# A gated long convolution with a feed-forward branch on one core: channel-innermost V and GC1, mixing and output in one block, the test on far lags turned round

## What is computed

```
proj = xn @ in_proj_w + in_proj_b
v = proj[..., :d]
for i in range(2):                         # two orders
    ctrl = proj[..., (i + 1) * d:(i + 2) * d]
    h = implicit_filter(...)               # a filter of 2048 lags per channel
    v = causal_conv(v, h)
    xc = conv3(ctrl); v = v * xc * sigmoid(xc @ gate_w[i] + gate_b[i])
attn = v @ out_proj_w + out_proj_b
r = relu(xn @ Wfc.T + gate * low_rank);  ffn = (r * r) @ Wproj.T
out = x + attn + ffn
```

## Time and profile before

| | |
|---|---|
| median of three runs | 960.2 us |
| profiled execution | 957.4 us, its span 955.8 us |
| mixing stage | about 372 to 870 us |
| output stage | about 870 to 956 us |
| TensorE busy | 863.9 us, 90% |
| VectorE, ScalarE busy | 631.3 us, 479.1 us |
| GpSimd busy | 248.7 us |
| DMA | 152.8 MB, mean 160 GB/s |

### The profile page before, as it was taken

The page is one execution under the profiler, slowest core; times in us unless marked ns, Lnnn a source line. Parts: engine busy times, 40 slices in busy tenths (PEclk is TensorE's granted clock), DMA queues, the critical chain, the costliest instruction groups (busy, mean ns, idle before and its releaser), DMA issues. The chain is left out here.

```text
span 955.8 us, 26466 instructions
## 1 busy us (share of the span) xinstructions
PE 863.9 (90%) x9972; PEld 718.4 (75%) x9973; DVE 631.3 (66%) x1025; ACT 479.1 (50%) x678; POOL 248.7 (26%) x268
## 2 busy tenths in 40 slices
PE   6846999999999973999999999999999999972995
PEld 3324888888888863888888888888888888862895
DVE  6882799898998973456555565565555655651885
ACT  5413677777777773333443343444434343334662
POOL 1022464664646601011121121111111111110111
PEclk9977899999999997999999999999999999985998
DMA  6272323324233129676778868778777687693897
GB/s 185 65 252 106 117 100 123 141 88 159 105 119 145 68 95 292 119 172 160 164 146 195 181 154 172 145 174 183 176 167 162 148 183 172 127 196 86 249 332 275
DMA packets 86705, 152.84 MB, mean 160 GB/s; under 512 B 12981, under 2 KB 62278, under 8 KB 85382
## 3 DMA queue, kind: packets, MB, share of 16 engines
q1 hardware_dynamic: 74902, 109.01, 47.2%
q0 software_dynamic: 11616, 42.21, 13.4%
q10 hardware_dynamic: 144, 1.05, 0.3%
HBM read 102.83 MB, written 49.41 MB: 159 GB/s over the span
## 5 line engine op out<-in xcount | busy, mean ns | idle before, releaser
L1080 PEld LDWEIGHTS py<-vwin,lead 64*64 64x64 f32 x5120 | 134.0, 134 | 35.8 <-issue 35.8
L965 DVE TENSOR_TENSOR r_lo<-r,r_hi 128x512 fp32r<-128x512 f32 x128 | 107.6, 840 | 78.8 <-ACT r_hi L1012 78.8
L1080 PE MATMUL py<-vwin,lead 64*64 64x128 f32 (+4 forms) x5120 | 147.8, 266 | 12.8 <-issue 12.7
L1012 ACT ACTIVATE r_hi<-r 128x512 fp32r<-128x512 f32 x128 | 80.8, 631 | 153.7 <-DVE r L960 153.7
L1009 ACT ACTIVATE r<-pf 128x512 f32<-128x512 f32 x128 | 76.5, 598 | 137.2 <-PE pf L412 132.7
L1061 PE MATMUL pp<-wproj,r_hi 128*128 128x256 f32 x512 | 135.9, 299 | 3.4 <-DVE r_lo L965 2.4
L1061 PE MATMUL pp<-wproj,r_lo 128*128 128x256 f32 x512 | 127.8, 282 | 0.0
L451 POOL TENSOR_SCALAR lead<-lead,norms 128x256 f32<-128x256 f32 x64 | 113.8, 1788 | 3.4 <-POOL norms L445 3.4
L1061 PEld LDWEIGHTS pp<-wproj,r_hi 128*128 128x128 f32 x512 | 96.9, 189 | 19.2 <-DVE r_lo L965 5.7
L611 DVE SCALAR_TENSOR_TENSOR xc<-ctrl,taps,xc 128x512 f32<-128x512 f32 x128 | 96.8, 776 | 18.8 <-ACT xc L683 18.1
L410 PE MATMUL pf<-tokens,split_a 128*128 (+1 forms) x256 | 101.3, 396 | 0.4 <-issue 0.4
(11 more groups left out here) (158 smaller groups left out, 1607.1 us busy)
## 6 DMA issues: line engine op xcount, KB each, us to landing
lead<-filters SPq DMA_DIRECT2D x128, 320.0 KB, 5.9
xnT_hbm<-split_b SPq DMA_DIRECT2D x32, 512.0 KB, 3.1
tokens<-xnT_hbm POOLq DMA_DIRECT2D x32, 512.0 KB, 7.0
lead<-in_attn_x SPq DMA_DIRECT2D x16, 512.0 KB, 3.8
gc_hbm<-xc SPq DMA_DIRECT2D x16, 512.0 KB, 2.6
xb<-in_attn_x POOLq DMA_DIRECT2D x16, 512.0 KB, 7.2
xf_hbm<-xb POOLq DMA_DIRECT2D x16, 512.0 KB, 3.8
GC<-gc_hbm SPq DMA_DIRECT2D x32, 256.0 KB, 7.4
```

What stands on the lines that cost most here:

```text
L965: dve.tensor_tensor(r_lo[j][:, :], r[j][:, :], r_hi[j][:, :].bitcast(F32), ALU.subtract).then_inc(r_split, 1)
L1012: act.activation(r_hi[j][:, :], r[j][:, :], ACT.Copy).then_inc(r_hi_done, 1)
L1080: last = pe.matmul(py[g % 2][q * BW:(q + 1) * BW, side, l, :, A:NB], tile[rows, q * PAIR + l, j * BW:(j + 1) * BW], vwin[g % 2][rows, q, l ...
```

## The change

`V` and `GC1` become [128, batch, block, channel slot 128]. The stores of the projection stage are then contiguous, the group accesses of the mixing stage touch single words 512 bytes apart (two adjacent channel slots on each of two sides). The copy to `ys` is gone: TensorE transposes straight out of `V`.

`output_stage` is gone as a block of its own; its code goes to the end of `mix_stage`, without a barrier. Its buffers are laid over others: `pT` over `py`, `po` over `pf` and `pp`, the halves of `wo` over the first token buffer, those of `yg` over `split_b` and the second token buffer, `yg` in `GC1`. New waits order that: `y_out`, `relu_done` and `xf_ready` on TensorE, `fc_mm` on ScalarE. VectorE's gate of chunk 0 goes ahead of the last `r_lo`. TensorE's loop over the output's chunks is unrolled.

`load_output` goes from behind the last T load to the start of the last chunk's four groups, ahead of the T load of group 60.

SP and TensorE test `tail < 1` and have the usual loops in the If branch.

```diff
@@ SP, T loads @@
+                        if g == 0 and isinstance(it, int) and it == NCH - 1:
+                            sp.wait_ge(y_out, GROUPS // ORDERS + 2)
+                            sp.wait_ge(xf_saved, 16 * SLOTS)
+                            load_output(sp)
                         if not first or g:
                             wait_alone(sp, group_mm, G + 1, sp_passed)
                             load(T[g % 2], 0, NEAR, T_loaded[g % 2])
...
-            with sp.If(tail > 0):
+            def stages(far):
                 for order in range(ORDERS):
-                    loads(order, True)
+                    loads(order, far)
+                sp.wait_ge(xf_saved, 16 * NCH)
+                for c in (SLOTS, SLOTS + 1):
+                    gates(c, c % SLOTS)
...
+            with sp.If(tail < 1):
+                stages(False)
             with sp.Else():
-                for order in range(ORDERS):
-                    loads(order, False)
-            sp.wait_ge(y_out, GROUPS // ORDERS + 2)
-            sp.wait_ge(xf_saved, 16 * SLOTS)
-            load_output(sp)
+                stages(True)
@@ mix_stage @@
-        Vs = V[:, :, :, :].rearrange("p (b c) n a -> p b c (n a)", b=SIDES)
-        Gs = GC1[:, :, :, :].rearrange("p (b c) n a -> p b c (n a)", b=SIDES)
+        Vs = V[:, :, :, :].rearrange("p n a (b c) -> p b c (n a)", b=SIDES)
+        Gs = GC1[:, :, :, :].rearrange("p n a (b c) -> p b c (n a)", b=SIDES)
@@ VectorE @@
+                    if last and g == GPI - 1:
+                        gated(0, 0)
                     low(it, 2 * g + 1)
...
+            yg_low(0, 0)
+            gated(1, 1)
             scale(NCH - 1)
             add(NCH - 1)
+            yg_low(1, 1)
+            for c in (2, 3):
+                output(c, c)
...
@@ TensorE @@
+            def stages(far):
+                for order in range(ORDERS):
+                    mixed(order, far)
+                pe.wait_ge(y_out, GROUPS + 2)
+                transposed(0, 0)
+                transposed(1, 1)
+                proj(NCH - 1, HT - 2)
+                proj(NCH - 1, HT - 1)
+                pe.wait_ge(wo_split, 1)
+                pe.wait_ge(relu_done, NCH * HT + 2)
+                projected(0, 0)
+                pe.wait_ge(xf_ready, NCH + 1)
+                for c in range(2, NCH):
+                    transposed(c, c % SLOTS)
+                    projected(c - 1, (c - 1) % SLOTS)
+                projected(NCH - 1, (NCH - 1) % SLOTS)
+
+            with pe.If(tail < 1):
+                stages(False)
+            with pe.Else():
+                stages(True)
```

More of the change, by code:

```diff
@@ L811, in channels, with mix_stage @@
     return m * (GPI * PAIR) + g * PAIR
[L814 removed]
+def mix_stage(nc, load_output, xf_saved, gc2_saved, x, filters, fc_hi, fc_lo, proj_t, xnT_hbm, xf_hbm, out_b, scales, flag, V, GC1, T, wfc, xm, split, T_loaded, w_in, xn_loaded, load_T, load_tokens,
+              out, load_gates, load_sum, ident, gc2, xf, wo, yg, gc2_loaded, xf_loaded, wo_in):
     with ExitStack() as ctx:
@@ L939, in _ @@
             save_xf(NCH - 1)
+            with pool.Fori(0, NCH // SLOTS) as m:
+                for j in range(SLOTS):
+                    c = m * SLOTS + j
+                    wait_alone(pool, out_ready, c + 3, pool_passed)
+                    pool.dma_start(out_tiles[bass.ds(c, 1)].rearrange("c p i d -> (c p) i d"), xf[j]).then_inc(out_saved[j], 16)
+            for j in range(SLOTS):
+                pool.wait_ge(out_saved[j], 16 * NCH // SLOTS)
         @block.vector
@@ L965, in low, with blocks, gated, yg_low @@
                 dve.tensor_tensor(r_lo[j][:, :], r[j][:, :], r_hi[j][:, :].bitcast(F32), ALU.subtract).then_inc(r_split, 1)
+            def blocks(rows):
+                return rows.rearrange("p k (t j) -> p k t j", j=BW)
+            def gated(c, j):
+                dve.wait_ge(yT_mm, c + 1)
+                dve.wait_ge(gc2_loaded[j], (c - j) * (16 * KT // SLOTS) + 16 * KT)
+                dve.tensor_tensor(blocks(yg[j % 2]), pT[j % 2].rearrange("p t k j -> p k t j"), blocks(gc2[j]), ALU.mult).then_inc(yg_ready, 1)
+            def yg_low(c, j):
+                i = j % 2
+                dve.wait_ge(yg_hi_done, c + 1)
+                dve.tensor_tensor(ygs[i][1], yg[i], ygs[i][0].bitcast(F32), ALU.subtract).then_inc(yg_split, 1)
+            def summed(c, j):
+                dve.wait_ge(out_mm, c + 3)
+                dve.wait_ge(xf_loaded[j], (c - j) * (16 // SLOTS) + 16)
+                dve.tensor_tensor(xf[j], po[j % 2], xf[j], ALU.add).then_inc(out_ready, 1)
+            def output(c, j):
+                gated(c, j)
+                summed(c - 2, (j + 2) % SLOTS)
+                yg_low(c, j)
             def body(order, m, it, first):
+                last = isinstance(it, int) and it == NCH - 1
                 for g in range(GPI):
@@ L984, in body @@
                     square(it, 2 * g + 1)
+                    if last and g == 1:
+                        dve.wait_ge(wo_hi_ready, 1)
+                        dve.tensor_tensor(wos[1], wo, wos[0].bitcast(F32), ALU.subtract).then_inc(wo_split, 1)
+                    if last and g == GPI - 1:
+                        gated(0, 0)
                     low(it, 2 * g + 1)
             for order in range(ORDERS):
-                lagging(dve, order, lambda m, it, first: body(order, m, it, first))
+                lagging(dve, order, lambda m, it, first: body(order, m, it, first), True)
+            yg_low(0, 0)
+            gated(1, 1)
             scale(NCH - 1)
             add(NCH - 1)
+            yg_low(1, 1)
+            for c in (2, 3):
+                output(c, c)
+            with dve.Fori(1, NCH // SLOTS) as m:
+                for j in range(SLOTS):
+                    output(m * SLOTS + j, j)
+            for c in (NCH - 2, NCH - 1):
+                summed(c, c % SLOTS)
         @block.scalar
@@ L1022, in body @@
                     activate(it, 2 * g)
+                    if last and order == ORDERS - 1 and g == 0:
+                        act.wait_ge(wo_in, 16 * KT)
+                        act.wait_ge(fc_mm, (NCH - 1) * HT + HT)
+                        act.activation(wos[0], wo, ACT.Copy).then_inc(wo_hi_ready, 1)
                     activate(it, 2 * g + 1)
@@ L1029, in _, with high @@
                 body(order, ITERS - 1, ITERS * order + ITERS - 1, True)
+            def high(c, i):
+                act.wait_ge(yg_ready, c + 3)
+                act.wait_ge(out_mm, c + 1)
+                act.activation(ygs[i][0], yg[i], ACT.Copy).then_inc(yg_hi_done, 1)
+            act.wait_ge(fc_mm, NCH * HT + HT)
+            with act.Fori(0, NCH // 2) as m:
+                for i in range(2):
+                    high(m * 2 + i, i)
         @block.tensor
```

209 lines of the change are left out of this document (49 added, 160 removed).

## The result

The changed kernel takes 974.4 us (median of four, 973.3 to 977.2) where the kernel before takes 959.9: ratio 1.0149, 95% interval 1.0111 to 1.0188. It is slower by 1.5%. I had forecast 958 and a range of 943 to 970.

The account below looks back on a forecast made before the run. TensorE was taken to bound the mixing, TensorE and DMA nearly level to bound the output, with a gap between. Terms -22.3 + 17.5 - 6 + 8.5 = -2.3 from 960.2 gave 958 us, range 943 to 970.

Parts of the forecast that it names:

- Part 1: Mixing and output joined without a barrier: matmuls of chunk 2 start 23.9 us earlier, -22.3 us in all, bounds -18 and -24.
- my list: Mixing's end: operations from the last V operation (849.80) to the last feed-forward add (861.0), then its save, landed about 865.
- At the 313 GB/s of the earlier trace that is 67 us: Joined output: 21.0 MB of loads and stores left after the last save take 67 us, so DMA ends at 935.
- Between the two I take 933.5: End of the joined output: taken between 935 by DMA and 931.9 by the compute pace, giving -22.3 us.
- Part 2: Output's inputs loaded ahead of group 60's T load: TensorE stands 16 us, plus 1.5 at low clock; +17.5 us.
- my sum: Ahead of group 60: from the moved load's first issue at 808.4 to group 60's T load landed at 838.5.
- rival (a): Group 60's T load isn't late, through queue order or a higher read rate; 940, or 949 with half the stall; chance 0.16.
- Part 3: Mixing's start: the usual loops fall through, without the 7.7 us branch; group 1 starts 6.5 us earlier; -6 us.
- Landing after 7.9 as the slowest T load, at 382: Mixing's start: T load of group 1, issued at about 374.5, lands at 382, so group 1 starts 6.5 us earlier.
- Part 4: V and GC1 with channel innermost: 0.5 us more per V operation, paid at 15 chunk closings; +8.5 us, bounds 0 and +19.
- Rival (c): Mixing's start keeps its stall, since the code behind the test isn't fetched ahead either; 964 us; chance 0.07.

Follow-up runs that it names:

- join alone: Changed kernel with the old layout, the old test and the slots loaded behind the last T load, so only the join remains: 944.0 us, ratio 0.9813.
- thin gates: Changed kernel with slots loaded behind the last T load and gate loads from chunk 4 on cut to an eighth of their bytes: 943.8 us, ratio 0.9821.
- layout alone: Kernel before with only the layout of V and GC1 changed, ys still copied: 969.9 us, ratio 1.0080.
- test alone: Kernel before with only the test turned round on TensorE and SP, usual loops in the If branch: 964.7 us, ratio 1.0014.

## Why the prediction failed, point by point

Sum: forecast -2.3, measured +14.5.

**Part 1, the join: -22.3 forecast, -18 +- 4 measured** (0.9813, join alone); in the traces -15.3 in after and -15.8 in the join alone, counted from group 63. The chain ahead of DMA came as worked out: the last add ends 10.7 us behind the last V operation (11.2 in my list), the save has landed after 14.2 (15.2), and the first store comes 24.1 us earlier (23.9). The step that failed is the term behind it, "At the 313 GB/s of the earlier trace rows that is 67 us". With 2.7 for the end, DMA was to take 70 us from the landed save on; in after it takes 76.5 (897.0 to 973.5), at a mean of 277 GB/s, since it starts at 225 (895 to 905), runs at 308 and ends at 186 (960 to 973). That is 7 us. "Between the two I take 933.5" took off 1.5 more, by a compute pace that no longer held. In after the stores of the chunks in the middle come 4.6 to 5.9 us apart instead of 4.26. The kernel before has the head start of its gap: its slots are loaded and the gates of three more chunks issued (by 888.65) when its first store goes out at 888.91. From 905 to 950 it also moves more than the joined kernels (335 GB/s against 308 in after and 317 in the join alone); no run shows why. That the bytes set the pace of the joined output is what the thin gates show.

**Part 2, the moved load: +17.5 forecast, +19.3 in the trace, 24 +- 5 by the ratios.** Right in mechanism and place; in size by the trace (16 and 1.5 forecast, 17.7 and 1.7 measured), while the ratios allow up to 6 more. From the first of the 14 issues to the start of group 60 it takes 31.3 us (821.39 to 852.72), 30.1 in my sum. No run separates the order in SP's queue from the sharing of the DMA engines. It is the largest single cost of the change, and rival (a), to which I gave 0.16, is out.

**Part 3, the test: -6 forecast, +1.3 +- 3 measured.** This step failed too, and by as much. "Landing after 7.9 as the slowest T load, at 382": it landed near 387. I took a landing time from the middle of the mixing and used it in the one place where the weights, two token chunks, two broadcasts and `xb` are all under way. (The T load of the same place in before lands after 6.0 to 7.2 us, but it is issued at 380.2, behind the others, which GpSimd issues from 372.2 to 378.6; in after they go out from 370.0 to 376.4 and the T load at 371.7, among them.) In after DMA is busy there from 372 to 387 (share 1.03), and T of group 1, issued 8 us earlier, lands about when it landed before. With the longer idle stretch (9.6 us) group 1 also runs at the low clock, 3.96 us for its weight loads instead of 2.07. With T loaded early the turned test brings 7.1 us against the kernel before, about what I had forecast.

**Part 4, the layout: +8.5 forecast, +7.7 measured.** Right by place (the closings) and size. The V operation was slowed by 0.67 and 0.39 us where I had 0.5 for both. A column costs 0.76 ns more with the output hopping and 1.32 with one input hopping too. The Trainium skill (Vector Engine (DVE) Microarchitecture Reference, 5.2 Measured stream behaviour) has 0.66 more for the output and 0.93 for all three streams, with hops of 4 KiB; the measured ones, with steps of 512 B, are larger, and they decide.

**The range.** It ended at 970 because the cost of each part was varied by itself. By the ratios the parts are -18.0, +24.0, +1.3 and +7.7, together +15.0 where +14.5 was measured: the start missed its forecast by 7 us, the join by 4 (7 in the traces), and the moved load by 6.5 (2 to 3 in the traces). The first two alone make 969 of the 958, all three 975; the range had no room for misses on the same side. Rival (c), the start keeps its stall, was the right one for the start and had 0.07; its reason was wrong, since the code was there in time (the test took 0.09 us and group 0 ran some 10 us earlier) and the data weren't.

**Left open.** In every kernel whose TensorE program was changed, groups 34 and 35 together take 2.0 to 4.0 us longer than in the kernel before, mostly as idle time with no releaser (2.1 us of it in one wait in after); with the layout alone it is 0.9. It comes in the first pass of order 1's loop. That it is code fetched at a new place is a guess; no run separates it. In the runs with the old layout groups 1 to 59 are together 1.9 to 6.9 us longer than in before, so the layout isn't the only cost there. How the ratios' 24 us and the trace's 19.3 for the moved load go together is open as well, within the intervals.

## What to carry to other kernels

Before moving a load ahead of another on the same queue, write down when the other one is wanted and how many bytes stand before it: here 4.46 MB ahead of a 0.65 MB load cost as much as removing a whole barrier brought, or more (19.3 against 15.3 us in the traces). A landing time holds only for the traffic in which it was read, so removing a stall on the issuing side was worth nothing here until the data could come sooner. And when stages are joined, look at what worked ahead in the gap (DMA here); cost the stage behind by that resource's bytes, with its slower start and end, and not by the old pace.

## What the runs showed of the hardware

Single words 512 B apart cost on three engines. VectorE: 0.39 us more for 512 columns written, 0.67 for written and read. ScalarE: 1.13 us instead of 0.62 for 512 columns read, 2.10 instead of 1.06 for 1024 written. TensorE: a weight load of a transpose 258 ns instead of 140. Runs of eight words cost nothing on VectorE, nor did single-word reads from PSUM at this step (`V<-pn` 1.21 us in both layouts). A taken branch over the far variant cost 7.7 us (before, ahead of the mixing), 8.1 (test alone, at the end of the mixing, 862.0) and 5.3 (after, near the end), the last two hidden.
